# One-hots of source rows in an RGCN kernel: four records' at once by one 16-bit comparison, in place of one comparison a record

## The reference

```python
def _rgcn_conv(x, edge_index, edge_type, W, root, bias):
    out = x @ root + bias
    for r in range(N_REL):
        mask = (edge_type == r).astype(x.dtype)
        s = segment_sum(x[src] * mask[:, None], dst)     # sum over edges into a node
        c = segment_sum(mask, dst)
        out = out + (s / maximum(c, 1.0)[:, None]) @ W[r]
    return out
# h = conv, relu, conv, relu, conv;  result = layernorm(x + h)
```

## Time and profile before

| | us |
|---|---|
| runs (3): median, lowest, highest | 2107.09, 2102.64, 2108.2 |
| the profiled execution's own time | 2101.77 |
| its span in the trace | 2099.9 |
| busy: TensorE / its weight loads | 1663.6 / 1191.4 |
| busy: VectorE / ScalarE / GpSimd | 1375.2 / 1141.7 / 1486.7 |
| L1504, 686 instructions, busy | 189.8 |
| L1505, 686 instructions, busy | 325.8 |

### The profile page before, as it was taken

How to read it: one execution, slowest core, us unless ns; L and a number is a source line. 1 busy time by engine, 2 the same in 40 slices (tenths; PEclk the granted TensorE clock), 3 DMA queues, 4 the chain that set the end, 5 groups by cost and what they waited for, 6 DMA issues and landing times.

```text
span 2099.9 us, 29766 instructions
## 1 busy us (share of the span) xinstructions
PE 1663.6 (79%) x8636; PEld 1191.4 (57%) x8636; DVE 1375.2 (65%) x4230; ACT 1141.7 (54%) x1679; POOL 1486.7 (71%) x1459
## 2 busy tenths in 40 slices
PE   6802657888889999769999889978769999997743
PEld 3402544554556666447876656655458777775532
DVE  4797866899999989424269887876234242446752
ACT  4511000244557788367858767777367676764500
POOL 1088777777777777657777777777467777777774
PEclk9955665799999999889999999999879999999855
DMA  6411222233344445387855444445488777763431
GB/s 202 158 35 34 73 62 64 82 126 103 119 141 137 166 170 187 127 277 251 263 160 170 158 144 164 166 152 171 138 272 259 238 246 242 245 213 108 139 89 49
DMA packets 169227, 330.81 MB, mean 158 GB/s; under 512 B 34704, under 2 KB 85648, under 8 KB 169060
## 3 DMA queue, kind: packets, MB, share of 16 engines
q1 hardware_dynamic: 119000, 230.27, 31.7%
q0 software_dynamic: 46400, 94.97, 16.1%
q10 hardware_dynamic: 3660, 3.60, 0.7%
HBM read 210.05 MB, written 118.65 MB: 157 GB/s over the span
## 4 chain that ended last, share of the span: by engine, by line
POOL 47%; PE 17%; issue 15%; DVE 14%; DMA 3%; DVEq 1%; ACT 1%; ACTq 1%; SPq 0%; POOLq 0%
POOL ring L794 44%; DVE V L1505 5%; PE psD L1043 4%; PE psB L1043 3%; DVE S L1452 3%; POOL rows L794 3%; PE psY L836 3%; DVE V L1504 3%; DMA ring<-ytab,idxc 2%; PE psGR L959 2%; PE psRB L959 1%; DVEq L1460 1%; PE psT L836 1%; DVE node L1474 1%; DMA hrows<-yst 1%
## 5 line engine op out<-in xcount | busy, mean ns | idle before, releaser
L794 POOL DMA_INDIRECT ring<-ytab,idxc x1402 | 1417.9, 1011 | 578.4 <-issue 420.5
L1043 PE MATMUL psD<-afull,xs 128*128 128x512 f32 (+1 forms) x1862 | 623.8, 462 | 29.0 <-ACT afull L1128 11.8
L1452 DVE TENSOR_SCALAR S<-odd_f,relc,wc 128x129 f32<-128x129 f32 x1450 | 480.6, 399 | 30.6 <-PE psGR L959 19.6
L1128 ACT ACTIVATE afull<-aring 128x1024 fp32r<-128x1024 f16 (+1 forms) x375 | 366.8, 1032 | 128.9 <-PE psD L1043 55.4
L1043 PEld LDWEIGHTS psD<-afull,xs 128*128 128x128 f32 (+1 forms) x1862 | 361.2, 198 | 95.0 <-ACT afull L1178 17.3
L1505 DVE TENSOR_SCALAR V<-odd_h,recs 128x513 f16<-128x513 f16 x686 | 325.8, 475 | 0.0
L1178 ACT ACTIVATE afull<-psT 128x512 fp32r<-128x512 f32 x355 | 205.6, 594 | 183.3 <-PE psT L1059 181.0
L959 PE MATMUL psRB<-S,ring 128*128 128x128 f32 (+1 forms) x1440 | 224.6, 305 | 96.6 <-DMA ring<-ytab,idxc 92.4
L1182 ACT ACTIVATE aring<-afull 128x1024 f16<-128x1024 f32 x275 | 286.1, 1040 | 25.5 <-ACT afull L1178 0.7
L959 PE MATMUL psGR<-S,ring 128*128 128x128 f32 x1364 | 215.3, 308 | 104.7 <-DMA ring<-ytab,idxc 93.6
L959 PEld LDWEIGHTS psRB<-S,ring 128*128 128x128 f32 (+1 forms) x1440 | 206.0, 214 | 125.3 <-issue 84.2
(11 more groups left out here) (207 smaller groups left out, 1610.9 us busy)
## 6 DMA issues: line engine op xcount, KB each, us to landing
aring<-a_dram SPq DMA_DIRECT2D x180, 512.0 KB
a_dram<-aring SPq DMA_DIRECT2D x132, 512.0 KB
ytab<-yst SPq DMA_DIRECT2D x144, 256.0 KB
ring<-ytab,idxc POOLq DMA_INDIRECT x1402
hrows<-yst SPq DMA_DIRECT2D x96, 64.0 KB
yst<-hrows SPq DMA_DIRECT2D x24, 256.0 KB, 4.8
yst<-in_x SPq DMA_DIRECT2D x23, 256.0 KB, 4.2
out<-yst SPq DMA_DIRECT2D x11, 256.0 KB, 2.7
```

The lines of the kernel that those rows point to most:

```text
L794: e.indirect_dma_start(rows_at(n, i, m), None, Y[li % 2], bass.IndirectOffsetOnAxis(ap=idxc[0:m, t:t + 1], axis=0)).then_inc(landed(n), 16)
L1043: last = e.matmul(bank[:], xs[0:m, s, i, :], a, start=(i == 0 and s == 0), stop=(i == NB - 1 and s == 1))
L1128: e.activation(afull[:, n % AF, 0:m, :], aring[:, cc % AS, o:o + m, :], ACT.Copy).then_inc(q["s_cv"], 1)
L1452: last = e.tensor_scalar(run3(S[:, n % NS, i, 0:P + 1]), odd128f, relc[:, t:t + 1], wc[:, t:t + 1], ALU.is_equal, ALU.mult)
```

## The change

The source one-hots of up to four successive records of a window (a batch) are made by one tensor_tensor comparison of 128 x 4 elements: the row number against the four records' rows, with the record as the innermost index. The records' source rows are kept in 16 bits (`recr`) for it, the keys stay in 32 (`reck`). The batches have a ring of NQ = 3 places of their own; the key one-hots keep theirs of six. TensorE reads a source one-hot from its batch with a step of four elements.

```diff
+    NQ = 3
...
+    batch_of, batches = {}, []
+    for v, (w, _, _) in enumerate(pairs):
+        if not batches or len(batches[-1]) == 4 or pairs[batches[-1][0]][0] != w:
+            batches.append([])
+        batch_of[v] = (len(batches) - 1, len(batches[-1]))
+        batches[-1].append(v)
...
-        recs = sb("recs", [P, 2, NSL])
+        recr, reck = sb("recr", [P, NSL], F16), sb("reck", [P, NSL])
...
-        oh = V[:, NR * P:NR * P + OH].bitcast(F16).rearrange("p (v c) -> p v c", v=NO)
-        ohs, ohk = oh[:, :, 0:P + 1], oh[:, :, P + 2:(1 + NR) * P + 3]
+        ohk = V[:, NR * P:NR * P + OH - NQ * 2 * P].bitcast(F16).rearrange("p (v c) -> p v c", v=NO)[:, :, 0:NR * P + 1]
+        ohs = V[:, NR * P + OH - NQ * 2 * P:NR * P + OH].bitcast(F16).rearrange("p (b c i) -> p b c i", b=NQ, i=4)
...
-                    e.matmul(tbank(u)[:], ohs[:, v % NO, 0:P], ohk[:, v % NO, 0:NR * P], start=(j == 0),
+                    e.matmul(tbank(u)[:], ohs[:, batch_of[v][0] % NQ, :, batch_of[v][1]], ohk[:, v % NO, 0:NR * P], start=(j == 0),
...
-                    if v >= NO:
-                        e.wait_ge(q["s_bd"], v - NO + 1)
                     at = pl.slot0[w] + i * pl.win[w][2] + j
-                    e.tensor_scalar(run3(ohs[:, v % NO, :]), odd128, recs[:, 0, at:at + 1], None, ALU.is_equal)
-                    e.tensor_scalar(run3(ohk[:, v % NO, :]), odd512, recs[:, 1, at:at + 1], None, ALU.is_equal
+                    used = v - NO + 1
+                    n, first = batch_of[v]
+                    if not first and n >= NQ:
+                        used = max(used, batches[n - NQ][-1] + 1)
+                    if used > 0:
+                        e.wait_ge(q["s_bd"], used)
+                    if not first:
+                        m = len(batches[n])
+                        e.tensor_tensor(ohs[:, n % NQ, :, 0:m], by4(irep[:, 0:4 * P])[:, :, 0:m],
+                                        recr[:, at:at + m].unsqueeze(1).to_broadcast([P, P, m]), ALU.is_equal)
+                    e.tensor_scalar(run3(ohk[:, v % NO, :]), odd512, reck[:, at:at + 1], None, ALU.is_equal
                                     ).then_inc(q["s_oh"], 1)
...
-                e.tensor_scalar(recs[:, :, o:o + n], psB[:, 0:2 * n].rearrange("p (a c) -> p a c", a=2), -1.0, None, ALU.add)
+                e.tensor_scalar(recr[:, o:o + n], psB[:, 0:n], -1.0, None, ALU.add)
+                e.tensor_scalar(reck[:, o:o + n], psB[:, n:2 * n], -1.0, None, ALU.add)
```

More of the change, by code:

```diff
@@ L111, in constants @@
         "c_odd": np.tile(odd_rows(P, np.float32), (P, 1)),
-        "c_odd16": np.tile(np.concatenate([odd_rows(P, np.float16), odd_rows(NR * P, np.float16)]), (P, 1)),
+        "c_odd16": np.tile(odd_rows(NR * P, np.float16), (P, 1)),
         "c_irep": np.tile(np.repeat(np.arange(max([P] + [c * pl.NB for _, _, c in pl.win]), dtype=np.float16), 4), (P, 1)),
@@ L420, in rgcn_kernel @@
         run3 = lambda z: z.rearrange("p (a c) -> p a c", a=3)
-        odd_f, odd_h = sb("odd_f", [P, P + 4]), sb("odd_h", [P, (1 + NR) * P + 8], F16)
-        odd128f, odd128, odd512 = rows3(odd_f[:], P), rows3(odd_h[:, 0:P + 4], P), rows3(odd_h[:, P + 4:], NR * P)
+        odd_f, odd_h = sb("odd_f", [P, P + 4]), sb("odd_h", [P, NR * P + 4], F16)
+        odd128f, odd512 = rows3(odd_f[:], P), rows3(odd_h[:], NR * P)
         irep = sb("irep", [P, 4 * max([P] + width)], F16)
@@ L459, in rgcn_kernel @@
         cnt = sb("cnt", [NR, P])
-        recs = sb("recs", [P, 2, NSL])
+        recr, reck = sb("recr", [P, NSL], F16), sb("reck", [P, NSL])
         WB = W * NB
-        OH = NO * ((1 + NR) * P + 4) // 2
+        OH = NO * (NR * P + 2) // 2 + NQ * 2 * P
         PBW = 12 * P + 4 * max(width)
```

## The result

The changed kernel takes 2096.93 us (median of 10 runs, 2093.23 to 2101.49), the kernel before beside it 2106.18 (2101.37 to 2108.51): ratio 0.9961 [0.995, 0.9973], 9.2 us or 0.4% faster.

The account below looks back on a forecast made before the run. GpSimd's stream of 1,450 gathers was taken as the bound. Holding +6.1, batches behind chains +2.2 and ring waits -2.9 gave +5.4 us on a median of 2107.1: 2112 us, range 2097 to 2124 (forecast's own 2104 to 2119).

Parts of the forecast that it names:

- What the saving is worth: Relieving VectorE ends five waits of GpSimd for ring places in layer 0: gain 2.9 us, nothing more.
- the 71 us: VectorE's net saving: 130 us of comparisons removed, 59 us of batch instructions added; 41 us of it in layer 0.
- 3.3 us either way: Chance spread of what 58 chains of `bins` cost, as they meet the gathers at other phases.
- The holding: New two-input batch instructions delay GpSimd's gathers: 34 ns an instruction, 6.1 us, plus 2.2 us behind chains of `bins`.
- the three values: Estimates of what the batch instructions hold: 3 us from below, 6.1 in the middle (taken), 30 from above.
- hold nearly nothing: Rival: lone batch instructions hardly delay gathers, giving 2107 to 2109 us; chance 0.26.
- the chains' ends: Eleven batches directly behind a chain of `bins` lengthen it by 0.33 us each, costing gathers 2.2 us.
- Odd slots: Rival: 90 batches read from odd slots lose the fast form, 0.69 us each, +8.4 us, 2121 us; chance 0.10.
- VectorE's pace: Rival: unprofiled runs have longer ring waits in layer 0, relief gains 16 against 8 of holding, 2099 us; chance 0.12.
- What would show it: Signs expected in the profile after: instruction counts and lengths, VectorE's load, ring waits, gather lengths and weight loads.
- I am wrong if: Gathers 0.94 us beside all new instructions, excess over 0.944 under 45 or over 70 us, or a turn changing over 2 us.

Follow-up runs that it names:

- e1: Changed kernel with the batch comparison as a tensor_scalar with one SBUF input, VectorE still relieved, source one-hots not the reference's: 2095.77 us, ratio to the kernel before 0.9934.
- after: The changed kernel itself, against the kernel before the change: 2096.93 us, ratio 0.9961.
- e2: Changed kernel plus two unread narrow comparisons a batch, so VectorE is about as loaded as in the kernel before: 2114.2 us, ratio to that kernel 1.0023.
- e3: Kernel before with ten places in the ring of gathered rows instead of nine, order of work unchanged: 2103.74 us, ratio to the kernel before 0.9974.
- e4: Changed kernel with every window's records beginning at an even slot: 2096.08 us, ratio to the kernel before 0.9932.
- the square: Four kernels, VectorE loaded or relieved, without or with the two-input batch instruction; ratios to before: 1 (before), 1.0023 (e2), 0.9934 (e1), 0.9961 (after).
- e10: The changed kernel run again, unaltered, on a chip where the kernel before takes 325 to 355 us longer: ratio to the kernel before 0.994.

## Why the prediction was wrong, by its own steps

**The step that failed is "What the saving is worth".** It says that 2.9 us of ring waits go and that "the rest of the 71 us lands on an engine that GpSimd doesn't wait for". The relief measured by itself is 13.9 us (e1) and 13.1 (after against e2). From before to e1 it has two parts:

- *Ring waits, 5.5 us in place of 2.9* (e3, interval 3.4 to 7.8). The size was read from one execution and taken for all. That execution was 4 to 5 us better than the median, by its holds ahead of 392 us as far as the traces tell.
- *Less holding beneath the chains of bins, 8 to 9 us* (47.8 to 39.4 in after, to 38.5 in e1), in place of nothing but chance. The spread of "3.3 us either way" supposed that the mean of a chain's hold stays what it was. In six profiles it stays with a full VectorE (before, e2, e3) and falls with a relieved one (e1, after, e4). That it goes with the relief is shown by e1 against e3 and e2 and by the nine profiles of the slower chips; how is only argued. Behind a held gather the next starts a fixed 0.82 + 0.30 us after the chain, so its phase is set by VectorE; what VectorE does up to the next chain, work back to back or a pause for TensorE, then decides how the gather meets it.

From e2 to after, 13.1 us, the first part is missing: neither profile has a ring wait. The gathers from 392 us on are some 11 us shorter there in sum, of which 3 us are the shorter unheld gather of after's execution. So the ring waits don't belong to VectorE's load alone, and the part of 5.5 us holds only beside the kernel before.

**The holding: right in kind, and near in size.** Lone batch instructions hold 10.0 us in after, against 6.1 forecast. One cause of the excess is the 0.55 us of the odd slots: by the same working they hold (0.55 - 0.13)^2 / 2.5 = 0.07 us each, and 84 x 0.070 + 85 x 0.034 = 8.8. The other is the gathers that start up to 0.07 us ahead of the instruction, which the working left out: 2.2 of the 10.0 us. With all at 0.42 (e4) they hold 5.4 us on 169, 32 ns each against the 34 worked out. That match is partly luck: with the starts ahead counted in, to 0.06 us, the working gives (0.42 - 0.06)^2 / 2.5 = 0.052, and e2's trace has 11.7 us where e4's has 5.4. Of the three values the middle was nearest, and "hold nearly nothing" was wrong, though 121 of the 169 lengthen no gather: the 48 that do pay for all. In time the second operand costs 4.9 to 5.7 us in the square, forecast 8.3 with the chains' ends, and nothing that shows in e4 against e1.

**Odd slots.** The rival had the address right and the price half: 0.55 us, not 0.69. The trace contradicts section 5.1 of the Vector Engine (DVE) Microarchitecture Reference of the Trainium skill for this access (four f16 of a batch repeated for 128 rows): at an odd slot it costs 0.13 us more, and e4 takes that back.

**VectorE's pace.** This rival was nearest in time, 2099, and it put the price of the relief at 16, measured 13.9. But its mechanism, 13 us of ring waits, is right for 5.5 of them only; with 5.5 in place of 16 against its 8.3 of holding it would have given 2110.

**SBUF — State Buffer, "Who interferes with whom",** in the Trainium skill infers that such instructions don't hold descriptor generation. The traces show that they do: 2.20 us in before, 1.39 beneath a lone one in after; and e2 is 4.9 us slower with them.

**What would show it.** L1504 gone and 179 instructions of the new kind: yes. VectorE in 392 to 842 us: 390.46, forecast some 380; the odd slots and one-hots built earlier fill it. No ring wait left: yes, but e2 has none either, so this sign didn't test the relief. Mean of the gathers up by 3 ns (1011 to 1014), forecast 5. Ends 0.8 behind single new instructions: yes. Excess between 45 and 70: 50.8; turns changed by less than 2 us: 1.6. Weight loads were forecast at 123 ns; the step of four costs 17 ns, not 23:

```profile
L1068 PEld LDWEIGHTS psT<-V 128*128 128x128 f16 x258 | 28.0, 117 | 54.4 <-issue 29.6 <-DVE V L1521 11.2 <-ACT afull L1187 9.2
```

None of the signs named as "I am wrong if" came, and still the sign was wrong: the excess over 0.944 was watched as one sum, in which the relief and the new holds cancel.

**What stays open.** In the traces, after's gathers from 392 us gain nothing (+0.8 us), so with the 5.5 of the ring 4.7 us of the 9.2 are accounted for; for e4 it is (-4.7 - 5.5) some 10 of 14.3, or 13 once the 2.9 us are added that its longer unheld gathers (0.946 us) make in that stretch. For e1 the same account closes within 2 us, but from an execution 10 us under its median; for e2 it closes if 2.9 us of longer unheld gathers and the 5.5 us of ring waits are taken off its 12.0. One profiled execution of each kernel, with turns that wander by 2 us, doesn't settle the rest.

## What to carry to other kernels

When an engine near its limit is relieved, don't take the waits of one execution, or the "other engine doesn't wait for it" as the worth of the relief. Test it by itself, with a kernel that has the relief without the new instruction, and one that has the instruction without the relief. Where gathers by GpSimd set the time, it is the length of unbroken runs of two-input VectorE instructions that costs, and more than in proportion to it. Put a one-input instruction between any two of them: here that took e4's 2096 us to 2065, with the same instructions, though on another chip. Split an excess by its causes before using it as a test.

## What the runs showed of the hardware that was not expected

- A broadcast comparison of 128 x 4 f16 takes 0.42 us when its four f16 begin at an even slot and 0.55 at an odd one. The 0.13 us is about one more cycle for each of 128 rows at 0.96 GHz (an estimate; the clock by the Trainium skill, Vector Engine (DVE) Microarchitecture Reference, 5.2).
- Five two-input instructions in a row hold gathers 0.65 to 0.94 us on average in layer 0; the same five apart some 0.27 over the program.
- A two-input instruction holds a gather that starts beneath it, and mostly (19 of 28) one that starts up to 0.075 us ahead of it, if it runs on beyond 0.13 us behind the gather's start; the gather then ends some 0.8 us behind the instruction. Of 15 that started 0.075 to 0.125 us ahead none was held.
- An unheld gather averages 0.944 us in 12 of the 20 profiled executions and 0.946 in the other 8, whatever the kernel and the chip. Over 1,450 gathers that is 3 us of the program.
- On three chips the kernel before takes 325 to 355 us longer, with the same instructions and, in e10's profile, gaps of up to 12.2 us before TensorE's weight loads.
